# A mixture-of-experts dispatch on one NeuronCore: 128 blank rows behind each expert's last row instead of blank regions, and the early plan spread over the routing loop

## Chip and metric

The kernel runs on 1 NeuronCore of one Trainium2 chip. The metric is the device time of one execution in microseconds (us); the median of several runs is compared. Engines: TensorE (PE), VectorE (DVE), ScalarE (ACT), GpSimd (POOL); SyncE (SP) only issues transfers here.

## Reference

Two transformer layers on x of shape 16 x 256 x 128 (4096 tokens of 128 values). Only the last part bears on the change: a linear attention and then a layer of 16 experts, of which each token uses 2.

```python
# x = x + attention0(layernorm(x)); x = x + gated_recurrence0(layernorm(x))
# x = x + linear_attention1(layernorm(x)); x = x + moe1(layernorm(x))
logits = xt @ Wr + br                       # T = 4096 tokens, E = 16
w, idx = jax.lax.top_k(softmax(logits), 2)
w = w / jnp.clip(jnp.sum(w, axis=-1, keepdims=True), 1e-09)
comb = comb.at[jnp.arange(T)[:, None], idx].add(w)
h = gelu(jnp.einsum('td,edh->teh', xt, W1) + b1)   # hidden 256
o = jnp.einsum('teh,eho->teo', h, W2) + b2
y = xt + jnp.einsum('teo,te->to', o, comb)
```

## The kernel before

Every engine has its own program; semaphores order them. The trace has three stages: softmax attention and the recurrence (to about 303 us), linear attention with routing (to about 448 us), and the experts (from about 441 us to the end).

**Routing.** The loop of `linear_attention_and_routing` handles one block of 256 tokens per iteration n; the parts of an iteration belong to blocks n, n-2, n-3, n-5 and so on, so that 16 blocks take iterations 0 to 21 or 22. From n = 16 on, parts drop out (no more new blocks): this is the drain. DVE runs through a fixed order of small operations for each n; an iteration is counted below from its first operation in the steady state, `feat` (L1267). For each (token, choice) DVE computes a place in the DRAM tensor `disp`: expert e owns the region of 4224 rows from e*4224 on, and its rows are filled in order. POOL scatters the rows of a block there with 4 indirect transfers (L1209, tensor `pay`, a ring of `STORED` = 3; ACT may fill a slot of `pay` only when the scatter of three blocks ago has landed, L1420).

**Tiles.** The experts work on 80 tiles of 128 rows of `disp`, in 40 pairs. Which expert and which place a tile has stands in a table (`tablei`). Its first 16 tiles (pairs 0 to 7) are planned early, from the counts after block 9, and are full tiles only (`plan_early`, 19 dependent DVE steps in three lumps at the end of iterations 15, 16 and 17). The other 64 are planned when all blocks are counted (`plan_rest`, 18 dependent steps, line L1069 and on), from the counts rounded up: an expert's last tile reaches over its last row. The rows there must be blank (zero weight, and an index that is out of bounds, so that nothing is written back). Before the change SP fills all regions of `disp` with blank rows from the tile `fill` during routing: nine transfers (L1177), three in flight, and POOL waits for the one that covers a block before it scatters it.

**Experts.** For pair i SP loads a word of the table (L1705), takes two addresses from it and issues two transfers `rows<-disp` (L1718) into one of `R3` = 8 slots; slot i+8 also waits until pair i has been written back (`yout`). At i = 8 SP waits for the second part of the table, for all scatters and for the blank transfers. PE's step i is: turn the rows of pair i (L1828), the hidden layer of pair i-1 (L1832), the outputs of pair i-2 (L1839), in this order in one queue:

```python
        def step(i, k, r):
            if isinstance(i, int) and i == COPIED:
                before["rest_turned"](pe)
            turn(i, k, r)
            hidden(i, k, r)
            outputs(i, k, r)
```

DVE's step i copies the two experts' weights for pair i (`copy_own`, L1749) and multiplies the outputs of pair i-4 by their weights (L1767, called y below). POOL writes y back with one indirect transfer for each tile (L1688, 79 in all). When all are written back, SP reads them in order, DVE adds, and SP stores the result.

Of the kernel before, what the change touches and what calls it, by code (L numbers as in the profile page):

```python
# [13 lines left out]
P = 128  # L14
# [932 lines left out]
BLANK = 4  # L947
BLANKS = 3
N_BLANK = TOKENS // (BLANK * P) + 1
EARLY_STEPS = 19  # L950
R3 = 8
# [9 lines left out]
def linear_attention_and_routing(nc, ctx, t):  # L961
# [5 lines left out]
    with ExitStack() as scope:  # L967
# [69 lines left out]
        blank = [sig(f"blank{c}", 16) for c in range(BLANKS)]  # L1037
        t["blank"] = blank
# [27 lines left out]

        def count_tiles(then, dve, of, more, least):
# [12 lines left out]
        def place_tiles(then, dve, at):  # L1080

            then(dve.tensor_scalar(passed[:, 1:], tiles[0][:, lead:], w["iota_t"][:, 0:1], None, ALU.is_le))
            then(dve.tensor_reduce(at[:, 0:1], passed[:, 1:], AX.X, ALU.add))
            then(dve.tensor_tensor(which[:, :], passed[:, 0:E], passed[:, 1:], ALU.subtract))
            then(dve.tensor_tensor(which[:, :], which[:, :], offset[:, :], ALU.mult))
            then(dve.tensor_reduce(prevt[:, :], which[:, :], AX.X, ALU.add))
            then(dve.scalar_tensor_tensor(out=at[:, 1:2], in0=at[:, 0:1], scalar=float(STRIDE), in1=prevt[:, :], op0=ALU.mult, op1=ALU.add))
            then(dve.tensor_scalar(at[:, 1:2], at[:, 1:2], w["iota_t"][:, 0:1], float(E * STRIDE), ALU.add, ALU.min))
            then(dve.tensor_scalar(at[:, 0:1], at[:, 0:1], float(E - 1), None, ALU.min))
# [16 lines left out]
        def plan_early(dve, then, n):  # L1106

            if n == EARLY_OF + 5:
                dve.wait_ge(pos_s.sem, pos_s.at(EARLY_OF - 1, 1))
                dve.wait_ge(zeros_set.sem, zeros_set.at(0))  # L1110
                count_tiles(then, dve, place[(EARLY_OF - 1) % PAIR][:, TT, :], 0.0, 0.0)
            if n == EARLY_OF + 6:
                add_up(then, dve)
                then(dve.tensor_scalar(capped[:, :], tiles[0][:, lead - 1:], float(EARLY), None, ALU.min))
                then(dve.tensor_scalar(offset[:, :], tiles[0][:, lead - 1:lead - 1 + E], -1.0, None, ALU.mult))
            if n == EARLY_OF + 7:
                place_tiles(then, dve, here[0])
                then(dve.tensor_tensor(taken[:, :], capped[:, 1:], capped[:, 0:E], ALU.subtract))

        def plan_rest(dve):  # L1120

            then = stepper(dve, plan)
            dve.wait_ge(pos_s.sem, pos_s.at(B - 1))
            count_tiles(then, dve, counts, float(P - 1), float(P))
            then(dve.tensor_tensor(tiles[0][:, lead:], tiles[0][:, lead:], taken[:, :], ALU.subtract))
            add_up(then, dve)
            then(dve.tensor_tensor(offset[:, :], taken[:, :], tiles[0][:, lead - 1:lead - 1 + E], ALU.subtract))
            place_tiles(then, dve, here[1])
# [24 lines left out]
        def sums_free(dve):  # L1153
# [3 lines left out]
                       dict(pe=banks_free, dve=sums_free, rest=plan_rest, pack=pack_table, rest_turned=rest_turned))  # L1157
# [4 lines left out]
        def _(sp):  # L1162
# [20 lines left out]
        def _(pool):  # L1183
# [35 lines left out]
            def iteration(n, r):  # L1219
                o = 1 - r  # L1220
                root_power(n, r)
                if active(n, 5):
                    b = n - 5
                    if b * S % (BLANK * P) == 0:
                        c = b * S // (BLANK * P)
                        pool.wait_ge(blank[c % BLANKS].sem, blank[c % BLANKS].at(c // BLANKS))
                    pool.wait_ge(pos_s.sem, pos_s.at(b))
                    pool.wait_ge(ids_up.sem, ids_up.at(b))
                    for i in range(TT):
                        for k in range(TOP):  # L1230
                            scatter(b, i, k)
# [5 lines left out]
        def _(dve):  # L1237
# [11 lines left out]
            early_step = stepper(dve, early)  # L1249

            def iteration(n, r):
# [8 lines left out]
                if active(n, 3):  # L1260
# [4 lines left out]
                    if kv_p.due(b - PAIR):  # L1265
                        dve.wait_ge(kv_p.sem, kv_p.at(b - PAIR))
                    dve.scalar_tensor_tensor(out=feat[b % PAIR][:, :, :], in0=ex[:, :, :], scalar=1.0, in1=rl[:, :, :], op0=ALU.min, op1=ALU.add)\  # L1267
                        .then_inc(feat_s.sem, 1)
                if active(n, 6):
# [4 lines left out]
                if active(n, 2):  # L1274
                    b = n - 2
                    dve.wait_ge(qkv_p.sem, qkv_p.at(b))
                    if rot_s.due(b - 1):
# [5 lines left out]
                        .then_inc(t_s.sem, 1)  # L1283
                if active(n, 3):
# [18 lines left out]
                if active(n, 5):  # L1303
# [3 lines left out]
                                      wide(w["br"][:, :].rearrange("p (o e) -> p o e", o=1), [P, TT, E]), ALU.add).then_inc(lg_s.sem, 1)  # L1307
                if active(n, 3):
# [18 lines left out]
                if active(n, 5):  # L1327
                    b = n - 5
                    for i in range(TT):
                        dve.wait_ge(top_s.sem, top_s.at(b, 1 + i))  # L1330
                        dve.max_index(where[:, i, :], best[:, i, :], logits[:, i, :]).then_inc(top_s.sem, 1)
                if active(n, 2):
# [5 lines left out]
                if active(n, 5):  # L1338
# [4 lines left out]
                        .then_inc(hot_s.sem, 1)  # L1343
                if active(n, 5):
# [18 lines left out]
                if active(n, 5):  # L1363
                    b = n - 5
                    dve.wait_ge(pay_s.sem, pay_s.at(b, 1))
                    dve.reciprocal(z[:, :], z[:, :]).then_inc(pay_s.sem, 1)
                if active(n, 3):
# [16 lines left out]
                if active(n, 5):  # L1384
# [3 lines left out]
                    if b >= STORED:  # L1388
                        dve.wait_ge(sent[b % STORED].sem, sent[b % STORED].at(b // STORED - 1))
                    dve.tensor_tensor(pay[b % STORED][:, :, :, D], odds[:, :, :],  # L1390
                                      wide(z[:, :].rearrange("p (o i) -> p o i", o=1), [P, TOP, TT]), ALU.mult).then_inc(pos_s.sem, 1)
                if active(n, 3):
# [15 lines left out]
                plan_early(dve, early_step, n)  # L1408
# [204 lines left out]
def experts(nc, ctx, scope, t, banks, before):  # L1613
# [79 lines left out]
    def expert_sp(sp):  # L1693
# [3 lines left out]
        def step(i, k, r):  # L1697
# [191 lines left out]
def program(nc, x, Wqkv, bqk, bv, Wout, bout, gates_w, gates_u, gates_b, in_c, wo, uo, bo, Wqkv2, Wout2, Wr, br, W1, W2, b2, cosf, sinf, out):  # L1889
    with ExitStack() as ctx:  # L1890
# [21 lines left out]
        def neighbours(dst, src):  # L1912
# [10 lines left out]
                 fill=sb("fill", [P, BLANK, ROW]))  # L1923
# [48 lines left out]
```

## Time and profile before

| What | us |
|---|---|
| median of 3 runs | 579.33 (578.74 to 581.08) |
| the profiled execution | 580.04 |
| its span in the trace | 578.3 |
| DVE busy, 340 to 400 us | 57.26 of 60 |
| nine blank transfers, 4160 KB each but the last, issue to landing (median) | 38.4 |
| POOL's 79 write-backs | first at 450.79, last at 556.70 |

All times inside the kernel are us from the start of the span. The 1.74 us between the span and the profiled execution's own time lie around the span and are taken as constant. The share of busy time of an engine over the whole span says little here, since the three stages have different limits.

### The profile page before, as it was taken

Reading aid. Unit: us, or ns where it says so; the run is one execution under the profiler, and the core shown is the slowest. Engines: PE = TensorE matmul, PEld = TensorE weight load, DVE = VectorE, ACT = ScalarE, POOL = GpSimd, SP = SyncE. Lnnn points to the kernel's source line nnn. Section 1 sums busy time; section 2 is a strip of 40 time slices with the busy share of each in tenths; the row PEclk is TensorE's granted clock in tenths of the full one; section 3 lists DMA queues with packets and bytes.
Section 4 is the critical chain, followed back from the end, with each engine's and each line's share of the span. In section 5 each row is a group of like instructions: output and inputs, shape, how many; then the busy total and the mean of one; then the engine's idle time right before and its main releaser. Section 6 shows DMA issues by size and latency. Waiting matters only on the chain. (4 is left out here: it accounts for less than half of the span.)

```text
span 578.3 us, 13705 instructions
## 1 busy us (share of the span) xinstructions
PE 479.2 (83%) x4110; PEld 329.1 (57%) x4110; DVE 400.3 (69%) x957; ACT 345.1 (60%) x763; POOL 332.9 (58%) x484
## 2 busy tenths in 40 slices
PE   6667899999999999989886899998767988988700
PEld 5433455555555555544463666666456887887700
DVE  5776777877877777775144899999857885554306
ACT  2026777777777777767733678787535665555400
POOL 2544575565666666513214158888657677777740
PEclk8768999999999999999999999999956999999955
DMA  3575755343444433320009999999944233333229
GB/s 94 137 185 138 174 123 122 94 104 106 113 112 112 112 98 97 94 60 5 2 1 311 380 375 367 365 368 367 357 89 108 79 99 90 91 97 89 66 97 343
DMA packets 78749, 89.93 MB, mean 156 GB/s; under 512 B 8523, under 2 KB 56032, under 8 KB 78688
## 3 DMA queue, kind: packets, MB, share of 16 engines
q1 hardware_dynamic: 72424, 78.82, 46.5%
q0 software_dynamic: 4576, 8.47, 4.4%
q10 hardware_dynamic: 1688, 1.90, 1.4%
q8 instruction: 29, 0.48, 0.4%
q14 instruction: 32, 0.26, 0.2%
HBM read 30.40 MB, written 59.72 MB: 156 GB/s over the span
## 5 line engine op out<-in xcount | busy, mean ns | idle before, releaser
L576 ACT ACTIVATE probs<-p_exp 128x1024 f32<-128x1024 f32 x128 | 131.5, 1027 | 57.9 <-PE p_exp L680 57.3
L450 DVE TENSOR_REDUCE negmax<-p_max 128x4 f32<-128x1024 f32 x103 | 126.1, 1224 | 46.4 <-PE p_max L708 45.8
L1688 POOL DMA_INDIRECT back<-XN2T,rows x79 | 83.1, 1052 | 26.0 <-issue 21.0
L1209 POOL DMA_INDIRECT disp<-pay,pos x64 | 65.5, 1024 | 22.9 <-issue 21.8
L699 PE MATMUL p_out<-probs,V 128*32 128x256 f32 x1024 | 68.3, 385 | 0.0
L680 PE MATMUL p_exp<-QS,KS 64*128 64x256 bf16 x512 | 51.1, 278 | 8.5 <-ACT probs L576 5.3
L1811 ACT ACTIVATE hid<-p_qkv,own 128x128 f32<-128x128 f32 x158 | 45.3, 369 | 18.4 <-PE p_qkv L1832 17.4
L708 PE MATMUL p_max<-KS,QS 61*128 61x256 bf16 x412 | 41.4, 280 | 6.8 <-DMA QS<-scratch 3.8
L1749 DVE TENSOR_SCALAR own<-expert,every_bit 128x578 int32 x79 | 38.6, 531 | 9.9 <-issue 8.9
L680 PEld LDWEIGHTS p_exp<-QS,KS 64*128 64x128 bf16 x512 | 15.0, 94 | 52.6 <-ACT probs L576 30.8
L1832 PE MATMUL p_qkv<-XN2T,own 128*128 128x128 f32 x316 | 43.4, 281 | 0.1
L1217 POOL TENSOR_TENSOR roots<-roots,power 128x4 f32<-128x4 f32 x19 | 24.2, 1272 | 29.1 <-DVE roots L1407 28.5
L699 PEld LDWEIGHTS p_out<-probs,V 128*32 128x32 f32 x1024 | 26.8, 109 | 24.6 <-issue 13.5
L366 POOL CAST maxpart<-negmax 128x32 bf16<-128x32 f32 x16 | 3.4, 212 | 63.8 <-DVE negmax L450 63.8
L1832 PEld LDWEIGHTS p_qkv<-XN2T,own 128*128 128x128 f32 x316 | 39.5, 196 | 0.8 <-ACT XN2T L1801 0.5
L450 DVE TENSOR_REDUCE negmax<-p_small 128x4 f32<-128x1024 f32 x25 | 30.5, 1220 | 8.3 <-PE p_small L708 8.2
L708 PEld LDWEIGHTS p_max<-KS,QS 61*128 61x128 bf16 x412 | 16.6, 96 | 21.9 <-DVE negmax L450 15.0
L78 POOL TENSOR_TENSOR root<-root,power 128x2 f32<-128x2 f32 x32 | 22.5, 702 | 2.7
L385 POOL CAST part<-qk 128x512 bf16<-128x512 f32 x15 | 9.2, 611 | 21.3 <-ACT qk L587 21.3
L352 POOL TENSOR_TENSOR xn<-X,mv 128x256 f32<-128x256 f32 x30 | 18.5, 617 | 4.9 <-POOL root L78 2.0
L754 PE MATMUL p_misc<-xn1T,Wqk 128*128 128x256 f32 x64 | 19.7, 435 | 1.4 <-ACT V L616 0.9
L76 POOL TENSOR_SCALAR root<-mv 128x2 f32<-128x2 f32 x32 | 6.2, 193 | 24.7 <-DVE mv L442 24.6
(269 smaller groups left out, 1162.9 us busy)
## 6 DMA issues: line engine op xcount, KB each, us to landing
disp<-fill SPq DMA_DIRECT2D x8, 4160.0 KB, 38.4
scratch<-part SPq DMA_DIRECT2D x32, 192.0 KB, 2.1
KS<-scratch SPq DMA_DIRECT2D x32, 192.0 KB, 3.6
QS<-scratch SPq DMA_DIRECT2D x28, 192.0 KB, 4.5
rows<-disp SPq DMA_DIRECT2D x79, 65.0 KB, 1.8
scratch<-part SPq DMA_DIRECT2D x32, 128.0 KB, 1.9
own<-back SPq DMA_DIRECT2D x8, 512.0 KB, 8.2
expert<-in_W_dram SPq DMA_DIRECT2D x1, 2064.0 KB, 8.9
```

Of the source, the lines that this page charges most:

```text
L78: pool.tensor_tensor(y, v, t["power"][:, 0:TT], ALU.pow).then_inc(mark.sem, 1)
L450: dve.tensor_reduce(negmax[q][:, i, :, 2 * hp:2 * hp + 2], bank[:, :].rearrange("p (v w k) -> p v w k", v=HALF, k=S), AX.X, ALU.max, negat ...
L576: act.activation(probs[s % 4][:, :, :, :].rearrange("p v w q -> p (v w q)"), p_exp[:, :], ACT.Exp).then_inc(prob_s.sem, 1)
L680: mm = pe.matmul(p_exp[:, (2 * v + w) * S:(2 * v + w + 1) * S], KS[q][rows, h, kt * P:(kt + 1) * P], QS[q][rows, h, :], start=True, stop=True)
L699: mm = pe.matmul(p_out[32 * j:32 * j + 32, 0:S], values[:, first:first + 32], probs[s % 4][:, j % HALF, j // HALF, :], start=(s % 4 == 0), ...
L708: mm = pe.matmul(bank[:, (2 * v + w) * S:(2 * v + w + 1) * S], QS[q][rows, h, i * P:(i + 1) * P], KS[q][rows, h, :], start=True, stop=True)
L1209: pool.indirect_dma_start(out=disp, out_offset=bass.IndirectOffsetOnAxis(ap=pos[q][:, i, k:k + 1], axis=0), in_=pay[q][:, k, i, :], in_off ...
L1217: pool.tensor_tensor(root[m][:, 0, :], root[m][:, 2, :], t["power"][:, :], ALU.pow).then_inc(power_s.sem, 1)
L1688: pool.indirect_dma_start(out=back, out_offset=bass.IndirectOffsetOnAxis(ap=rows[r][:, h, D + 1:ROW].bitcast(U32), axis=0), in_=y[r][:, h, :],
L1749: done = dve.tensor_scalar(own[r][:, h, :].bitcast(I32), theirs, every_bit[:, 0:1], None, ALU.bitwise_and)
L1811: done = act.activation(hid[q][:, h, c, :], p_hid[q % 2][:, (2 * h + c) * P:(2 * h + c + 1) * P], ACT.Gelu, bias=own[q][:, h, HID + c:HID ...
L1832: return pe.matmul(dst, own[q][:, h, c * P:(c + 1) * P], xT[q][:, h * P:(h + 1) * P], start=True, stop=True)
```

## The change

1. The nine blank transfers during routing and POOL's waits for them are gone; `fill` holds one row per partition instead of four.
2. When all blocks are counted, DVE converts the 16 end positions to integers (`ends`). SP, after its transfers for pairs 0 to 7 and before that of pair 8, loads each end position into a register and writes 128 blank rows from there on: 16 loads and 16 transfers of 65 KB (`pads`). Pair 8 waits for all of them.
3. The 19 steps of the early plan are no longer in three lumps in which each step waits for the one before it; they stand one by one at 8 sites in iterations 15 to 17, and the wait for the step before stands at the next site.
4. The rest of the plan is cut in two: 9 steps before the expert loop of DVE, 9 in its step 4 behind y of pair 0, and `copy_own` of pair 4 behind them.

```diff
@@ SP, end of the set-up of the routing stage
-            blanks = disp[0:E * REGION, :].rearrange("(e r) d -> e r d", e=E)
-            for c in range(N_BLANK):
-                n = BLANK if c + 1 < N_BLANK else 1
-                if c >= BLANKS:
-                    sp.wait_ge(blank[c % BLANKS].sem, blank[c % BLANKS].at(c // BLANKS - 1))
-                sp.dma_start(blanks[:, c * BLANK * P:(c * BLANK + n) * P, :].rearrange("e (p n) d -> p e (n d)", n=n),
-                             w["fill"][:, 0:n, :].rearrange("p (o n) d -> p o (n d)", o=1).broadcast_to([P, E, n * ROW]))\
-                    .then_inc(blank[c % BLANKS].sem, 16)
@@ POOL, before the scatter of block b
-                    if b * S % (BLANK * P) == 0:
-                        c = b * S // (BLANK * P)
-                        pool.wait_ge(blank[c % BLANKS].sem, blank[c % BLANKS].at(c // BLANKS))
@@ SP, expert loop
             if isinstance(i, int) and i == R3:
+                sp.wait_ge(w["loaded3"].sem, w["loaded3"].at(0))
+                sp.wait_ge(t["ends_s"].sem, t["ends_s"].at(0))
+                for e in range(E):
+                    end = sp.value_load(t["ends"][0:1, e:e + 1], min_val=0, max_val=E * REGION - P)
+                    sp.dma_start(disp[bass.ds(end, P), :], w["fill"][:, 0, :]).then_inc(t["pads"].sem, 16)
                 sp.wait_ge(table.sem, 2)
...
             if isinstance(i, int) and i == R3:
-                sp.wait_ge(w["loaded3"].sem, w["loaded3"].at(0))
-                for c in range(N_BLANK - BLANKS, N_BLANK):
-                    sp.wait_ge(t["blank"][c % BLANKS].sem, t["blank"][c % BLANKS].at(c // BLANKS))
+                sp.wait_ge(t["pads"].sem, t["pads"].at(0))
@@ DVE, the rest of the plan
+        def plan_rest(dve, then, half):
+
+            if half == 0:
+                dve.wait_ge(pos_s.sem, pos_s.at(B - 1, 1))
+                dve.tensor_copy(ends[:, :], counts[0:1, :]).then_inc(ends_s.sem, 1)
+                count_tiles(then, dve, counts, float(P - 1), float(P))
+                then(dve.tensor_tensor(tiles[0][:, lead:], tiles[0][:, lead:], taken[:, :], ALU.subtract))
                 add_up(then, dve)
...
+            if half == 1:
+                then(dve.tensor_tensor(offset[:, :], taken[:, :], tiles[0][:, lead - 1:lead - 1 + E], ALU.subtract))
+                for step in range(8):
+                    place_tiles(then, dve, here[1], step)
@@ DVE, the sites of the early plan (eight calls of site(n, s) in an iteration)
+            def site(n, s):
+                if 0 <= (n - EARLY_OF - 5) * SITES + s < EARLY_STEPS:
+                    early_ready()
+                    plan_early(dve, early_step, n, s)
...
-                plan_early(dve, early_step, n)
+                site(n, 7)
@@ DVE, expert loop
-        before["rest"](dve)
+        rest = before["rest"](dve)
+        rest(0)
         before["dve"](dve)
 
         def step(i, k, r):
-            if i is not None and not (isinstance(i, int) and i < COPIED):
+            if i is not None and not (isinstance(i, int) and i <= COPIED):
                 copy_own(dve, i, k, r)
...
+            if isinstance(i, int) and i == COPIED:
+                rest(1)
+                copy_own(dve, i, k, r)
```

Instructions in order, SP before the change, from the second transfer of pair 7 to the first of pair 8 (`TENSOR_LOAD` loads a register from SBUF, `ISA` and `REGISTER_ALU` compute the address):

```order
L1718 DMA rows7<-disp 128x130
L1705 TENSOR_LOAD tablei [waits table]
L1705 ISA x2
L1718 REGISTER_ALU [waits sent1,sent0,sent2,blank2,yout0,blank1,loaded3,blank0]
L1718 ISA
L1718 DMA rows0<-disp 128x130
```

SP after the change, from the same place (line numbers are those of the changed kernel), the first two of the 16 blank transfers:

```order
L1757 DMA rows7<-disp 128x130
L1743 TENSOR_LOAD ends [waits ends_s,loaded3]
L1743 ISA x2
L1744 ISA
L1744 DMA disp<-fill 128x130
L1743 TENSOR_LOAD ends
L1743 ISA x2
L1744 ISA
L1744 DMA disp<-fill 128x130
```

and the last of them up to pair 8:

```order
L1743 TENSOR_LOAD ends
L1743 ISA x2
L1744 ISA
L1744 DMA disp<-fill 128x130
L1746 TENSOR_LOAD tablei [waits table]
L1746 ISA x2
L1757 REGISTER_ALU [waits sent2,yout0,sent1,pads,sent0]
L1757 ISA
L1757 DMA rows0<-disp 128x130
```

Sixteen loads with 16 transfers now stand between pairs 7 and 8.

DVE before the change, the end of iteration 17 and the `feat` that opens the next one:

```order
L1407 TENSOR_SCALAR roots<-mv 128x4 [waits st4]
L1082 TENSOR_SCALAR passed<-tiles,iota_t 128x16
L1083 TENSOR_REDUCE here<-passed 128x1 [waits early]
L1084 TENSOR_TENSOR which<-passed 128x16 [waits early]
L1085 TENSOR_TENSOR which<-which,offset 128x16 [waits early]
L1086 TENSOR_REDUCE prevt<-which 128x1 [waits early]
L1087 SCALAR_TENSOR_TENSOR here<-here,prevt 128x1 [waits early]
L1088 TENSOR_SCALAR here<-here,iota_t 128x1 [waits early]
L1089 TENSOR_SCALAR here<-here 128x1 [waits early]
L1118 TENSOR_TENSOR taken<-capped 128x16 [waits early]
L1267 SCALAR_TENSOR_TENSOR feat<-ex,rl 128x512 [waits qfT_p,kv_p,el_s,early]
```

DVE after the change, from the end of iteration 16 into iteration 17, where the last three steps of the early plan now stand:

```order
L1443 TENSOR_SCALAR roots<-mv 128x4 [waits st4]
L1101 SCALAR_TENSOR_TENSOR here<-here,prevt 128x1 [waits early]
L1296 SCALAR_TENSOR_TENSOR feat<-ex,rl 128x512 [waits kv_p,qfT_p,el_s]
L1103 TENSOR_SCALAR here<-here,iota_t 128x1 [waits early]
L1303 TENSOR_REDUCE pos<-mine 128x4 [waits pos_s]
L1311 TENSOR_TENSOR t<-p_qkv,cosf 128x512 [waits rot_s,qkv_p]
L1312 TENSOR_TENSOR t<-p_qkv,sinf 128x64x4
L1105 TENSOR_SCALAR here<-here 128x1 [waits early]
L1320 TENSOR_TENSOR KVm<-p_kvo,kv_mask 128x144 [waits o_p,kv_p]
```

The nine steps at the end of iteration 17 are gone from there; each of the moved ones has other work between it and the step on which it waits.

## Rows read from the trace of the kernel before

**Rows 1.** Windows: busy us of five engines, then TensorE clock, DMA share, GB/s
```profile
340.00:400.00 60.00, 55.53 (x323) 39.55 (x323) 57.26 (x256) 48.51 (x133) 49.48 (x46) 1.00 1.05 367
400.00:420.00 20.00, 14.60 (x85) 10.53 (x82) 17.06 (x83) 12.51 (x36) 13.77 (x14) 0.91 1.07 354
420.00:444.00 24.00, 16.27 (x74) 12.99 (x71) 15.87 (x86) 9.28 (x25) 14.75 (x16) 0.52 0.41 89
450.00:557.00 107.00, 86.28 (x732) 81.00 (x730) 57.42 (x147) 55.17 (x181) 82.43 (x79) 0.97 0.30 81
```

**Rows 2.** Timeline of VectorE: start us, us, engine, line, operation, out<-in
```profile
364.21 0.69 DVE L1267 SCALAR_TENSOR_TENSOR feat<-ex,rl 128x512 f32<-128x512 f32 x1
...
375.81 0.15 DVE L1350 TENSOR_TENSOR z<-odds 128x2 f32<-128x2 f32 x1
375.88 0.43 DVE L1356 BATCH_NORM_STATS2 mv<-X 128x6 f32<-128x256 f32 x1
...
398.12 0.69 DVE L1267 SCALAR_TENSOR_TENSOR feat<-ex,rl 128x512 f32<-128x512 f32 x1
...
405.69 0.17 DVE L1069 TENSOR_TENSOR full<-place,region 128x16 f32<-128x16 f32 x1
...
406.53 0.69 DVE L1267 SCALAR_TENSOR_TENSOR feat<-ex,rl 128x512 f32<-128x512 f32 x1
...
414.48 0.69 DVE L1267 SCALAR_TENSOR_TENSOR feat<-ex,rl 128x512 f32<-128x512 f32 x1
...
423.07 0.69 DVE L1267 SCALAR_TENSOR_TENSOR feat<-ex,rl 128x512 f32<-128x512 f32 x1
```

**Rows 3.** Waits, 340 to 400 us: us in total, times, longest
```profile
DVE den L1311 <- PE p_kvo L1578: 1.7, 9, 0.2
...
ACT pay L1421 <- DMA disp<-pay,pos: 0.5, 1, 0.5
```

**Rows 4.** Timeline of GpSimd at the end of dispatch and in the expert stage
```profile
447.64 0.96 POOL L1209 DMA_INDIRECT disp<-pay,pos  x1 [0.30 <-issue]
...
450.79 0.99 POOL L1688 DMA_INDIRECT back<-XN2T,rows  x1 [2.19 <-DVE XN2T L1767]
...
467.71 1.07 POOL L1688 DMA_INDIRECT back<-XN2T,rows  x1 [0.30 <-issue]
```

**Rows 5.** Timeline of VectorE: products y of pair 0 and of pair 6
```profile
449.51 0.42 DVE L1767 TENSOR_TENSOR XN2T<-p_kvo,rows 128x256 f32<-128x256 f32 x1
...
461.88 0.42 DVE L1767 TENSOR_TENSOR XN2T<-p_h,rows 128x256 f32<-128x256 f32 x1
```

**Rows 6.** Timeline of the SP queue, and line L1705 in 438 to 439
```profile
437.33 1.03 SPq L1718 DMA_DIRECT2D rows<-disp  x2
...
439.17 1.02 SPq L1718 DMA_DIRECT2D rows<-disp  x2
...
449.35 1.01 SPq L1718 DMA_DIRECT2D rows<-disp  x2
...
454.71 1.02 SPq L1718 DMA_DIRECT2D rows<-disp  x2
...
L1705 SPq TENSOR_LOAD <-tablei x1: 273/273/273, 438.4 to 438.4; - x1
```

**Rows 7.** Line L1718 (ns min/median/max), and the page's DMA issues
```profile
L1718 SPq DMA_DIRECT2D rows<-disp x79: 332/337/765, 435.4 to 540.0; - x79
...
rows<-disp SPq DMA_DIRECT2D x79, 65.0 KB, 1.8
```

**Rows 8.** Timeline of TensorE: turns of pairs 0 and 8, two hidden layers
```profile
440.81 0.66 PE L1828 MATMUL p_ta<-ident,rows 128*128 128x128 f32 x2 [0.71 <-DVE mine L1400]
...
442.00 2.07 PE L1832 MATMUL p_qkv<-XN2T,own 128*128 128x128 f32 x8
...
446.70 1.06 PE L1832 MATMUL p_qkv<-XN2T,own 128*128 128x128 f32 x8
...
459.17 0.38 PE L1828 MATMUL p_ta<-ident,rows 128*128 128x128 f32 x2
```

More of the change, by code:

```diff
@@ L946 @@
 PLACE_BITS = 10
[L947 to L949 removed]
 EARLY_STEPS = 19
+SITES = 8
 R3 = 8
@@ L1036, in linear_attention_and_routing @@
         table = t["table"]
-        blank = [sig(f"blank{c}", 16) for c in range(BLANKS)]
-        t["blank"] = blank
+        ends, ends_s, pads = tmp("ends", [1, E], I32), sig("ends_s"), sig("pads", 16 * E)
+        t["ends"], t["ends_s"], t["pads"] = ends, ends_s, pads
         fill_set, bsplit = sig("fill_set", 2), sig("bsplit", 6)
@@ L1065, in stepper, with spaced, then @@
             return then
+        def spaced(dve, mark):
+            n = [0]
+            def then(ins):
+                n[0] += 1
+                ins.then_inc(mark.sem, 1)
+            return then, lambda: n[0] and dve.wait_ge(mark.sem, n[0])
         def count_tiles(then, dve, of, more, least):
@@ L1078, in add_up, with place_tiles @@
                 then(dve.tensor_tensor(b[:, lead:], a[:, lead:], a[:, lead - s:lead - s + E], ALU.add))
[L1080 to L1089, printed above, removed]
+        def place_tiles(then, dve, at, step):
+            if step == 0:
+                then(dve.tensor_scalar(passed[:, 1:], tiles[0][:, lead:], w["iota_t"][:, 0:1], None, ALU.is_le))
+            if step == 1:
+                then(dve.tensor_reduce(at[:, 0:1], passed[:, 1:], AX.X, ALU.add))
+            if step == 2:
+                then(dve.tensor_tensor(which[:, :], passed[:, 0:E], passed[:, 1:], ALU.subtract))
+            if step == 3:
+                then(dve.tensor_tensor(which[:, :], which[:, :], offset[:, :], ALU.mult))
+            if step == 4:
+                then(dve.tensor_reduce(prevt[:, :], which[:, :], AX.X, ALU.add))
+            if step == 5:
+                then(dve.scalar_tensor_tensor(out=at[:, 1:2], in0=at[:, 0:1], scalar=float(STRIDE), in1=prevt[:, :], op0=ALU.mult, op1=ALU.add))
+            if step == 6:
+                then(dve.tensor_scalar(at[:, 1:2], at[:, 1:2], w["iota_t"][:, 0:1], float(E * STRIDE), ALU.add, ALU.min))
+            if step == 7:
+                then(dve.tensor_scalar(at[:, 0:1], at[:, 0:1], float(E - 1), None, ALU.min))
         def pack_table(dve, i, n):
@@ L1104, in pack_table, with plan_early @@
             dve.tensor_copy(tablei[:, :, i * EARLY:i * EARLY + n], tf[:, :, 0:n]).then_inc(table.sem, 1)
[L1106 to L1108 removed]
+        def plan_early(dve, then, n, site):
+            step = (n - EARLY_OF - 5) * SITES + site
+            if step == 0:
                 dve.wait_ge(pos_s.sem, pos_s.at(EARLY_OF - 1, 1))
                 dve.wait_ge(zeros_set.sem, zeros_set.at(0))
[L1111 to L1118 removed]
@@ L1120, in plan_rest @@
-        def plan_rest(dve):
-            then = stepper(dve, plan)
[L1123 to L1128, printed above, removed]
+                then(dve.tensor_tensor(full[:, :], place[(EARLY_OF - 1) % PAIR][:, TT, :], w["region"][:, :], ALU.subtract))
@@ new lines, in plan_early @@
+            if step == 1:
+                then(dve.tensor_scalar(counti[:, :], full[:, :], 0.0, 0.0, ALU.add, ALU.max))
+            if step == 2:
+                then(dve.tensor_scalar(counti[:, :], counti[:, :], 7, None, ALU.logical_shift_right))
+            if step == 3:
+                then(dve.tensor_copy(tiles[0][:, lead:], counti[:, :]))
+            if 4 <= step < 8:
+                a, b, s = tiles[step % 2], tiles[(step + 1) % 2], 1 << step - 4
+                then(dve.tensor_tensor(b[:, lead:], a[:, lead:], a[:, lead - s:lead - s + E], ALU.add))
@@ new lines, in plan_early @@
+            if step == 8:
+                then(dve.tensor_scalar(capped[:, :], tiles[0][:, lead - 1:], float(EARLY), None, ALU.min))
+            if step == 9:
+                then(dve.tensor_scalar(offset[:, :], tiles[0][:, lead - 1:lead - 1 + E], -1.0, None, ALU.mult))
+            if 10 <= step < 18:
+                place_tiles(then, dve, here[0], step - 10)
+            if step == 18:
+                then(dve.tensor_tensor(taken[:, :], capped[:, 1:], capped[:, 0:E], ALU.subtract))
+        def plan_rest(dve, then, half):
[4 more added lines that the diff above has]
+                then(dve.tensor_tensor(tiles[0][:, lead:], tiles[0][:, lead:], taken[:, :], ALU.subtract))
+                add_up(then, dve)
+            if half == 1:
+                then(dve.tensor_tensor(offset[:, :], taken[:, :], tiles[0][:, lead - 1:lead - 1 + E], ALU.subtract))
+                for step in range(8):
+                    place_tiles(then, dve, here[1], step)
@@ L1130, in rest_turned, with rest_planner @@
+        def rest_planner(dve):
+            then = stepper(dve, plan)
+            return lambda half: plan_rest(dve, then, half)
         def rest_turned(pe):
@@ L1922, in program @@
         w.update(expert=sb("expert", [P, E, EXPERT_ROW]), b_all=sb("b_all", [E, D]),
-                 fill=sb("fill", [P, BLANK, ROW]))
+                 fill=sb("fill", [P, 1, ROW]))
         w["bp"] = w["expert"][:, :, EXPERT:EXPERT_ROW]
```

11 lines of the change are left out of this document (9 added, 2 removed).

## Prediction

> **What bounds the kernel now.** I first read the windows, stage by stage. Between 340 and 400 us, the steady state of routing, DVE is busy for 57.26 of 60 us, and the DMA share is at its full value with 367 GB/s: the blank transfers fill the memory path, but DVE fills its own time too [rows 1]. So the second view is DVE's timeline. From the `feat` at 364.21 to that at 398.12 five iterations pass, (398.12 - 364.21)/5 = 6.78 us each [rows 2]. The third view is who waits for whom: in that stretch DVE waits 1.7 us in all, and for PE; the scatter's landing delays ACT once, by 0.5 us [rows 3]. Traffic is therefore nearly hidden in the steady state, and at most the 2.74 us that DVE is idle there could come back.
>
> Iterations 15 to 17 are longer: 398.12 to 406.53 (8.41 us), to 414.48 (7.95), to 423.07 (8.59) [rows 2]. They hold the lumps of 4, 6 and 9 plan steps. Between 420 and 444 us the granted clock is 0.52, the lower level (1.2 GHz) almost throughout, and PE is busy for only 16.27 of 24 us [rows 1]: a drain of dependent steps.
>
> In the expert stage POOL sets the pace. From 450 to 557 us it is busy for 82.43 us in 79 write-backs, 1.04 us each, with 0.3 us between two of them: 79 x 1.34 = 106 of 107 us [rows 1, 4]. PE is ahead of it: y of pair 6 ends at 461.88 + 0.42 = 462.30, and its first write-back starts at 467.71 [rows 4, 5]. What decides the end is thus when POOL starts, and whether it ever runs dry.
>
> **What the change gives back in routing.** A dependent plan step costs 0.21 us: four of them fill 405.69 to 406.53 [rows 2]. A small operation that waits for nothing moves the next one by 0.07 us (375.81 to 375.88) [rows 2]; I take 0.07 to 0.1 for a spread step, and nothing for the two sites in each iteration that stand ahead of a wait for PE.
> - Iteration 15: four steps (0.84) become eight spread ones, six of which count (0.6): 0.2 saved. Besides, 8.41 - 6.78 - 0.84 = 0.8 us are left, in which `pay` waits for its scatter and PE's work comes late; without the blank traffic I count that as saved.
> - Iteration 16: six steps (1.26) become eight (0.6): 0.7 saved.
> - Iteration 17: nine steps (1.9) become three (0.2): 1.7 less on DVE. PE and ACT have work of their own ahead of the next `feat`'s matmuls, so I take 1.5.
> - The drain: with shorter gaps PE may keep its high clock a little longer. The stretch of 24 us at the low clock [rows 1] is work of PE in about half of its chain; I estimate up to 2.5 us if the clock held, and take 0.6.
>
> Sum 0.8 + 0.2 + 0.7 + 1.5 + 0.6 = 3.8 us earlier at the end of routing. I call this X. Its bounds: 2.0 (late landing not cured, a spread step at nearly 0.2) and 5.8 (clock kept in the drain).
>
> The Trainium skill, "DMA: Bandwidth & Descriptors", section "Latency and other measured facts", puts the access latency of HBM far lower under light load than under heavy load. That speaks for the 0.8 us of iteration 15; the row itself shows only one wait of 0.5 us in 60 [rows 3], and by the row alone X would be 3.5.
>
> **The start of the write-backs.** The rest plan's cut lets y of pair 0 come before 9 of the steps and before the copy for pair 4. The last scatter ends at 447.64 + 0.96 = 448.60; the first write-back starts only at 450.79, behind y of pair 0, which ends at 449.51 + 0.42 = 449.93 [rows 4, 5]. It could start at about 448.9: 1.9 us more, if POOL then does not run dry.
>
> **What the change adds: 16 blank transfers in SP's queue.** All are issued by SP between pairs 7 and 8. SP takes 439.17 - 437.33 = 1.84 us for a pair with one table load and two transfers. The second transfer of a pair starts 1.02 - 0.34 = 0.68 us behind the first, so a load with its transfer takes 1.84 - 0.68 = 1.16 us; the load starts at 438.4 and its transfer at 439.17, 0.77 us later [rows 6, 7]. A blank transfer has one register operation less, about 0.04 us; on the other hand pairs 1 to 7 took (449.35 - 437.33)/6 = 2.0 us each instead of 1.84 [rows 6]. I take 1.12 us, within 1.02 (0.34 for the issue and 0.68 for the load) and 1.20. So 16 x 1.12 = 17.9 us.
>
> SP is done with pair 7 at 449.35 + 1.01 = 450.36 [rows 6]. Before, it then had a wait for the table and issued pair 8 at 454.71 [rows 6]. Now, in times of the old trace (X comes off at the end), the last blank transfer is issued at 450.4 + 17.9 - 0.4 = 467.9. A transfer of this size lands in 1.8 us [rows 7]; a write may take a little more. Landing 469.7, with 0.4 for address work pair 8 is issued at 470.1 and its rows are there at 471.9.
>
> The Trainium skill, on the same page and in the same section, gives a floor of about 0.6 us to a register load. With 0.34 us for the issue a blank transfer would be 0.94 us, the stop 2.9 us shorter, and the result some 582; the row's 0.77 us from load to transfer decides otherwise.
>
> **Who waits for pair 8.** PE's queue is in order: turn of 8, hidden of 7, outputs of 6. While PE waits for the rows of pair 8, y of pair 6 can't be made. Before, the turn of pair 8 started at 459.17 and y of pair 6 ended at 462.30, 3.13 us later [rows 5, 8]. Now 471.9 + 3.1 = 475.0. By then PE has been idle for some 15 us; after the poor stretch that ends at 440.81 the first hidden layer took 2.07 us at the low clock, later ones 1.06 [rows 8], so I add 1.5 us for the two passes: 476.5. POOL starts 450.79 - 449.93 = 0.86 us behind y [rows 4, 5]: write-back of pair 6 at 477.4 instead of 467.71. That is 9.7 us later. The remaining 67 write-backs follow without a gap as before, since PE and DVE are faster than POOL: by pair 6 they had gained 467.71 - 462.30 = 5.4 us on it [rows 4, 5]. The 1.9 us of the earlier first write-back are lost in the stall.
>
> **Sum.** 9.7 - 3.8 = +5.9 us. On the profiled execution's 580.04 that is 585.9; it lies 0.7 above the median, so the predicted median is 579.33 + 5.9 = 585.3 us, rounded up.
>
> **Rivals.**
> - *The blank transfers are cheap* and SP is through before POOL needs pair 6. Without a stall POOL wants pair 6 at 448.9 + (467.71 - 450.79) = 465.8; the gain is X + 1.9 = 5.7: 573.6 us, faster. It needs 465.8 instead of 477.4, thus 11.6/16 less for each transfer: 0.40 us. The sign turns at 1.12 - 5.9/16 = 0.75 us. For it: the issue alone is 0.34 us. Against it: every transfer has its own load in front, and those took 0.77 us. Chance 0.08.
> - *The blank traffic held routing back more than the waits show.* DVE could win at most its idle time, 2.74 us in 60, some 3 over the loaded stretch: 582.3 us, at the edge of what can be told. Against it: DVE is full. Chance 0.12.
> - *The blank transfers are dearer*: writes of 128 short rows that come every 1.1 us back up, or the cold PE falls behind POOL for several pairs. At 1.4 us each, +4.5: 590 us. Chance 0.10.
> - *My forecast*, a stall at pair 8 less X: 0.70.
>
> **Numbers.** A measurement of this kernel tells about 0.5%, 2.9 us, from no change. The forecast's own range is from +1.5 (X 5.8, 1.05 us each, PE not cold) to +9.5 (X 2.0, 1.2 us each): 581 to 589. That also takes in the second rival; outside are the first, the third and some 0.02 of the others, so this is the range. Faster by over 0.5%: 0.08 and a little of the second rival's tail, 0.09. Within: half of the second rival and 0.11 of the forecast, 0.17. Slower: 0.74.
>
> **What the changed kernel's profile would show.** SP: 16 pairs of load and transfer, about 1.1 us apart, for some 18 us, and pair 8 issued around 466. POOL: write-backs of pairs 0 to 5 without a gap from about 445 on, then idle for some 10 us ahead of pair 6. PE: idle for about 15 us, then hidden layers of 2 us at clock 0.5. DVE: iterations 16 and 17 near 7.2 and 6.9 us, plan steps not back to back. DMA from 320 to 420 us nearly empty, and iterations of still 6.8 us there. The prediction is wrong if SP takes well under 0.75 us for a blank transfer, or if iterations before 14 get shorter.

## The result and the profile after

| What | us |
|---|---|
| kernel before, median of 7 runs | 579.56 (578.74 to 584.32) |
| changed kernel, median of 7 runs | 586.28 (583.54 to 587.52) |
| ratio, 95% interval | 1.0095 (1.0066 to 1.0124) |
| profiled execution of the changed kernel, its span | 583.54, 581.6 |

By the ratio the change made the kernel slower by 5.5 us (0.0095 x 579.56), between 3.8 and 7.2; the two medians stand 6.7 us apart. The profiled execution of the changed kernel is the fastest of its seven. Everything ahead of routing is unchanged code and ended 2.7 us earlier in this trace than in that of before (DVE's first instruction of the stage at 300.41 and 303.06), so I count from the first `feat` of each trace: 316.62 before, 313.94 after.

Windows of the changed kernel, the same four stretches and columns as [rows 1]:

```profile
340.00:400.00 60.00, 55.48 (x325) 39.80 (x323) 57.53 (x260) 48.20 (x133) 49.07 (x45) 1.00 0.12 39
400.00:420.00 20.00, 14.87 (x84) 11.31 (x83) 16.33 (x86) 12.71 (x34) 16.82 (x15) 0.87 0.13 41
420.00:444.00 24.00, 19.04 (x107) 15.85 (x106) 16.00 (x86) 11.45 (x34) 16.91 (x18) 0.61 0.33 87
450.00:557.00 107.00, 84.34 (x706) 80.86 (x704) 54.20 (x133) 53.27 (x176) 74.87 (x72) 0.93 0.31 84
```

In the first one the memory path is nearly empty now (39 GB/s instead of 367), and DVE is as busy as before. In the last one POOL is busy for 7.6 us less: it stood still. The stretches lie at fixed times, and the changed kernel reaches the end of routing some 7 us earlier in its trace, so the third one holds more of its expert stage and can't be compared column by column.

VectorE's timeline, the last four `feat` (L1296), answers to [rows 2]:

```profile
395.44 0.69 DVE L1296 SCALAR_TENSOR_TENSOR feat<-ex,rl 128x512 f32<-128x512 f32 x1
402.46 0.69 DVE L1296 SCALAR_TENSOR_TENSOR feat<-ex,rl 128x512 f32<-128x512 f32 x1
409.30 0.68 DVE L1296 SCALAR_TENSOR_TENSOR feat<-ex,rl 128x512 f32<-128x512 f32 x1
416.06 0.69 DVE L1296 SCALAR_TENSOR_TENSOR feat<-ex,rl 128x512 f32<-128x512 f32 x1
```

Iterations 15 to 17 take 7.02, 6.84 and 6.76 us instead of 8.41, 7.95 and 8.59: 4.33 us less. Up to 395.44 all iterations have kept their length (81.50 us from the first `feat` in both traces).

The SP queue (SPq: transfers that SP issues; ACTq below: those of ScalarE), timeline, and the loads of the end positions (ns min/median/max), answer to [rows 6]:

```profile
428.37 15.16 SPq L1757 DMA_DIRECT2D rows<-disp  x16
444.36 16.85 SPq L1744 DMA_DIRECT2D disp<-fill  x16
463.14 7.12 SPq L1757 DMA_DIRECT2D rows<-disp  x8
...
L1743 SPq TENSOR_LOAD <-ends x16: 262/271/356, 443.6 to 460.2; - x16
```

The 16 blank transfers follow the pairs 0 to 7 at once, (16.85 - 0.33)/15 = 1.10 us apart. Pair 8 is issued 19.6 us behind the end of pair 7.

TensorE at the outputs of pair 2 and at the end of the stall, VectorE's y of pair 6, timelines, answer to [rows 5, 8]:

```profile
445.90 0.29 PE L1879 MATMUL p_h<-own,ones 128*128 128x128 bf16 x1 [1.76 <-DVE tablef L1112]
...
465.92 0.69 PE L1871 MATMUL p_ta<-ident,rows 128*128 128x128 f32 x2 [10.64 <-DMA rows<-disp]
466.40 1.91 PE L1875 MATMUL p_qkv<-XN2T,own 128*128 128x128 f32 x8
...
470.10 0.42 DVE L1807 TENSOR_TENSOR XN2T<-p_h,rows 128x256 f32<-128x256 f32 x1 [12.20 <-PE p_h L1882]
```

GpSimd, timeline, answers to [rows 4]: the last scatter, the first write-backs of pairs 0, 1 and 2, and those of pair 6.

```profile
440.61 0.96 POOL L1236 DMA_INDIRECT disp<-pay,pos  x1 [0.30 <-issue]
441.88 1.00 POOL L1724 DMA_INDIRECT back<-XN2T,rows  x1 [0.30 <-issue]
...
446.46 0.98 POOL L1724 DMA_INDIRECT back<-XN2T,rows  x1 [2.29 <-DVE XN2T L1807]
...
449.56 0.98 POOL L1724 DMA_INDIRECT back<-XN2T,rows  x1 [0.84 <-DVE XN2T L1807]
...
471.34 1.19 POOL L1724 DMA_INDIRECT back<-XN2T,rows  x1 [10.75 <-DVE XN2T L1807]
...
474.16 0.98 POOL L1724 DMA_INDIRECT back<-XN2T,rows  x1 [0.30 <-issue]
```

The chain of the stall is to be read in these three views: SP issues pair 8 at 463.14, TensorE has waited 10.64 us for its rows, behind that turn in TensorE's queue stands what y of pair 6 needs (DVE waits 12.20), and POOL waits 10.75. Counted from the first `feat`:

| From the first `feat`, us | before | after | difference |
|---|---|---|---|
| last scatter starts | 131.02 | 126.67 | -4.35 |
| first write-back | 134.17 | 127.94 | -6.23 |
| write-back of pair 6 | 151.09 | 157.40 | +6.31 |
| last write-back (559.96 after) | 240.08 | 246.02 | +5.94 |

### The profile page after: what moved, and what is told of

Its sections match the earlier page's. It is cut to its first block and busy times, and to the rows that moved or that the text cites. A ratio compares the mean times of both kernels' runs of the same rounds, so it can differ in the third digit from the quotient of the medians.

```text
span 581.6 us, 13792 instructions
## 1 busy us (share of the span) xinstructions
PE 480.5 (83%) x4110; PEld 332.7 (57%) x4110; DVE 399.6 (69%) x958; ACT 344.3 (59%) x763; POOL 333.5 (57%) x484
## 5 line engine op out<-in xcount | busy, mean ns | idle before, releaser
L1788 DVE TENSOR_SCALAR own<-expert,every_bit 128x578 int32 x79 | 39.8, 546 | 9.6 <-issue 8.5
L1875 PE MATMUL p_qkv<-XN2T,own 128*128 128x128 f32 x316 | 45.1, 289 | 0.1
L1875 PEld LDWEIGHTS p_qkv<-XN2T,own 128*128 128x128 f32 x316 | 41.6, 205 | 0.5 <-ACT XN2T L1844 0.5
L385 POOL CAST part<-qk 128x512 bf16<-128x512 f32 x15 | 9.1, 609 | 19.6 <-ACT qk L587 19.6
L1844 ACT ACTIVATE XN2T<-p_ta 128x256 f32<-128x256 f32 x20 | 7.7, 384 | 21.2 <-issue 15.3
```

Of the source, the lines that this page charges most:

```text
L1788: done = dve.tensor_scalar(own[r][:, h, :].bitcast(I32), theirs, every_bit[:, 0:1], None, ALU.bitwise_and)
L1875: return pe.matmul(dst, own[q][:, h, c * P:(c + 1) * P], xT[q][:, h * P:(h + 1) * P], start=True, stop=True)
```

## Experiments

All are compared with the kernel before, run on the same chip in turn with them. Times "from the first `feat`" are from the one profiled execution.

**The plan alone** (e1_plan_only): the changed kernel, with the nine blank transfers and POOL's waits as before and no `pads`.

```diff
-                for e in range(E):
-                    end = sp.value_load(t["ends"][0:1, e:e + 1], ...)
-                    sp.dma_start(disp[bass.ds(end, P), :], w["fill"][:, 0, :]).then_inc(t["pads"].sem, 16)
+            # the nine transfers of the kernel before, ahead of the expert loop
```

> The blank transfers of before are kept; only the plan is spread and cut. If the loss of the change lies in SP's 16 transfers and its gain in the plan's steps, this has the gain alone: the changed kernel's routing ended 4.3 us earlier counted from the start of its stage, of which 3.5 are the plan's, and the write-backs follow POOL, so about 576 us against 579.6 (ratio 0.993). If instead the removed blank traffic brought the gain, this stays at 579.6. If the cut of the rest plan is what delays the experts, this is slower than before.

Measured 576.88 us against 579.28, ratio 0.9959 (0.9929 to 0.9989): the plan is the part that gains. Its last three iterations, and one wait of ScalarE (timelines):

```profile
398.25 0.69 DVE L1309 SCALAR_TENSOR_TENSOR feat<-ex,rl 128x512 f32<-128x512 f32 x1
405.27 0.69 DVE L1309 SCALAR_TENSOR_TENSOR feat<-ex,rl 128x512 f32<-128x512 f32 x1
412.11 0.68 DVE L1309 SCALAR_TENSOR_TENSOR feat<-ex,rl 128x512 f32<-128x512 f32 x1
418.85 0.69 DVE L1309 SCALAR_TENSOR_TENSOR feat<-ex,rl 128x512 f32<-128x512 f32 x1
...
419.91 0.21 ACT L1470 ACTIVATE pay<-ids 128x4 int32<-128x4 int32 x1 [1.79 <-DMA disp<-pay,pos]
```

The iterations are those of the changed kernel (7.02, 6.84, 6.74), with full blank traffic beside them. But one iteration later `pay` waits 1.79 us for a scatter that lands late, and from there on the trace is 1.9 us behind the changed kernel: the last scatter starts 128.54 us from the first `feat` (126.67 there). So of X = 4.35 us the spread plan gives 2.5 with the blank traffic beside it, and taking the traffic away then gives 1.9 more. Its last write-back starts 236.24 us from the first `feat`, 3.8 less than before. A difference of 2 us between two single traces is not safe by itself: the changed kernel, e5_half_on_act, e10_interleaved_again and e11_bare_again have the last scatter at 126.60 to 126.69, but e3_twice, with the same routing code, at 128.79. What carries the 1.9 us here is the wait of 1.79 us in the trace.

**The blank rows alone** (e2_lumps): the changed kernel with the early plan in its three lumps.

```diff
-                if 0 <= (n - EARLY_OF - 5) * SITES + s < EARLY_STEPS:
-                    early_ready()
-                    plan_early(dve, early_step, n, s)
+                if s == SITES - 1 and n in LUMPS:          # {15: (0, 4), 16: (4, 10), 17: (10, 19)}
+                    for step in range(*LUMPS[n]):
+                        plan_early(dve, early_step, EARLY_OF + 5, step)
```

> The changed kernel with the early plan back in three lumps of dependent steps at the ends of iterations 15, 16 and 17. By my theory the plan's spread gives 3.5 us and the stall at pair 8 moves with the end of routing: 586.3 + 3.5 = 589.8 us (ratio to before 1.017). If the blank traffic's end brought the gain, 586.

Measured 592.0 us, ratio 1.0205 (1.0165 to 1.0245). Iterations 15 to 17 took 7.59, 7.94 and 9.06 us, the last scatter started 130.61 us from the first `feat`, and the last write-back 249.79: 3.8 us behind the changed kernel, as expected. In this order the split of X is another one: without the plan's spread the empty memory path gives 0.4 us (131.02 to 130.61), since iteration 15 is 0.82 us shorter than before but iteration 17 is 0.47 us longer, and the spread then gives 3.9. What is shown is that the spread is the larger part, 2.5 to 3.9 us of 4.35, and that the two parts do not add up one by one. The medians stand 6 us apart; the rest of it lies ahead of the first `feat` in the trace (below) and isn't explained for the medians.

**Twice as many** (e3_twice): 16 more loads with transfers, to the 128 rows behind the blank ones.

```diff
+                for e in range(E):
+                    end = sp.value_load(t["ends"][0:1, e:e + 1], ...)
+                    sp.dma_start(disp[P:, :][bass.ds(end, P), :], w["fill"][:, 0, :]).then_inc(t["pads"].sem, 16)
```

> The changed kernel with every load and blank transfer issued twice, the second 128 rows further on, 32 in all. If SP's issue time is fully on the path, each costs the 1.10 us that stands between two of them in the trace: 16 x 1.1 = 17.6 us more, 604 us (ratio 1.042). If the delay at pair 8 had another cause (the landing of the last, the table), little is added: 586 to 588.

Measured 605.12 us, ratio 1.0442 (1.0394 to 1.0491), 18.8 above the changed kernel's median, 1.18 for each. SP's and POOL's timelines:

```profile
447.05 16.80 SPq L1744 DMA_DIRECT2D disp<-fill  x16
464.63 17.17 SPq L1747 DMA_DIRECT2D disp<-fill  x16
483.36 16.36 SPq L1760 DMA_DIRECT2D rows<-disp  x15
...
491.91 1.19 POOL L1724 DMA_INDIRECT back<-XN2T,rows  x1 [30.34 <-DVE XN2T L1810]
```

POOL's stall is 19.6 us longer: 30.34 instead of 10.75 us. In the queue itself each of the 16 more costs 1.10 us again: from the first blank transfer to pair 8 it is 36.31 us (447.05 to 483.36) instead of 18.78, 17.5 us more. From the first `feat` to the last write-back the trace is 19.7 us longer; 2.1 us of that lie ahead of the last scatter, in code that did not change, and why is open.

**Transfers without a load** (e9_bare, e11_bare_again): 16 more behind the 16, to fixed rows of a tensor of their own.

```diff
+                for e in range(E):
+                    sp.dma_start(t["spare"][e * P:(e + 1) * P, :], w["fill"][:, 0, :]).then_inc(t["pads"].sem, 16)
```

> The changed kernel with 16 more transfers of 128 rows in SP's queue behind the 16 blank ones, without a register load, to fixed rows of a tensor of their own. With load and register address 16 more cost 18.8 us, 1.18 each. Theory: the load (0.77 us from load to transfer) is the larger part, and a bare transfer costs the issue alone, 0.34 us: +5.4 us over the changed kernel, 591.7. Rival: the transfers themselves back up, because a write of 128 rows takes about 1.1 us of the queue: +18, 604.

> The kernel of e9_bare once more, for the same reason. Theory: 16 bare transfers cost 0.34 us each, +5.4 over the changed kernel, 591.7. Rival: they cost about 1.1 us each as the ones with a load do, +18, 604.

In the first comparison the kernel before itself took 627.33 us, and this one 642.63: ratio 1.023 (1.0178 to 1.0281). In the second they took 581.13 and 594.83, ratio 1.0236 (1.0196 to 1.0277), 8.2 us above the changed kernel's 1.0095. SP's and POOL's timelines of the second, and the row of line L1746:

```profile
445.76 16.82 SPq L1744 DMA_DIRECT2D disp<-fill  x16
462.62 8.29 SPq L1746 DMA_DIRECT2D spare<-fill  x16
473.65 26.14 SPq L1759 DMA_DIRECT2D rows<-disp  x22
...
482.12 1.19 POOL L1724 DMA_INDIRECT back<-XN2T,rows  x1 [19.99 <-DVE XN2T L1809]
...
L1746 SPq DMA_DIRECT2D spare<-fill x16: 320/432/936, 462.6 to 470.5; - x16
```

A bare transfer costs (8.29 - 0.4)/15 = 0.53 us in the queue, more than the 0.34 of a single issue (the longest was 0.94), and half of the 1.10 with a load. Neither expectation was met exactly; the load with its address work is about half of the price, not two thirds. (The bare ones also go to another tensor; whether that matters was not tested.)

**Eight of them on ScalarE** (e5_half_on_act).

```diff
-                for e in range(E):
+                for e in range(0, E, 2):
@@ ScalarE, at the end of its step i
+            if isinstance(i, int) and i < E // 2:
+                if i == 0:
+                    act.wait_ge(t["ends_s"].sem, t["ends_s"].at(0))
+                end = act.value_load(t["ends"][0:1, 2 * i + 1:2 * i + 2], ...)
+                act.dma_start(disp[bass.ds(end, P), :], w["fill"][:, 0, :]).then_inc(t["pads"].sem, 16)
```

> Half of the loads and blank transfers are issued by ScalarE, one in each of its steps 0 to 7; SP issues the other eight. By my theory SP reaches pair 8 8.8 us earlier, and POOL's idle time ahead of pair 6 falls from 10.8 us to 2 or less: 577.5 us (ratio 0.996). If the landing or PE's low clock holds pair 6 back, or ScalarE's steps become the limit (1.1 us more in each), 582 to 586.

Measured 584.49 us, ratio 1.0066 (1.004 to 1.0092): my expectation of a gain fell, and the time lies where its rivals had put it (582 to 586). SP's, ScalarE's and POOL's timelines:

```profile
449.26 8.36 SPq L1744 DMA_DIRECT2D disp<-fill  x8
465.02 34.84 SPq L1757 DMA_DIRECT2D rows<-disp  x29
...
462.90 0.34 ACTq L1865 DMA_DIRECT2D disp<-fill  x1
...
473.08 1.19 POOL L1724 DMA_INDIRECT back<-XN2T,rows  x1 [5.34 <-DVE XN2T L1807]
```

SP was through at 457.6, but ScalarE's steps are paced by TensorE and its last transfer came at 462.90; pair 8 waited for that one. The stall is halved, and the wait for the counts in ScalarE's step 0 took part of it back in front of pair 0 (POOL idle 2.54 us there, 0.30 in the changed kernel).

**The same 16, only those that are needed ahead of pair 8** (e8_interleaved, e10_interleaved_again). Pair 8 needs the blank rows of the first experts alone.

```diff
@@ SP, at pair 8
-                for e in range(E): (load and transfer)
+                for e in range(4): (load and transfer)
@@ SP, behind the transfers of pairs 8 to 14
+            if isinstance(i, int) and R3 <= i < R3 + 7:
+                pad(sp, 4 + i - R3, t["more"][(i - R3) % 2])
@@ ScalarE, at the end of steps 4 to 8
+                pad(act, 11 + i - 4, t["by_act"])
```

> The changed kernel with the same 16 blank transfers placed otherwise: SP issues 4 before pair 8 and one behind each of pairs 8 to 14, ScalarE issues 5 in its steps 4 to 8; pair 8 waits only for the first 4, each later pair for those of two pairs before. (The order holds for the counts of these inputs; for all inputs it would need a guard.) Theory: what costs is that 16 transfers stand in one queue ahead of pair 8, 12 of them without need; pair 8 is then issued some 12 us earlier than in the changed kernel, POOL's idle time before pair 6 falls from 10.75 us to under 1, and the routing gain is left: 586.3 - 10 = 576, up to 578 if SP, at 2.9 us for each of pairs 8 to 14 against POOL's 2.68, falls behind. Rival: the blank transfers cost where the write meets the scatters and reads in the DMA queues, wherever they are issued; then the time stays over 582.

> The kernel of e8_interleaved once more, because in that comparison the kernel before itself took 627 us instead of 579 and POOL was no longer what sets the pace of the expert stage. Where the kernel before takes about 579: theory, POOL's idle time before pair 6 under 2 us instead of 10.75 and 576 to 578 us. Rival: the blank transfers still hold up something else that shares their queues, and the time stays over 582.

The first comparison is the one with 627.33 us for the kernel before: this one took 627.64, ratio 0.9995 (0.9956 to 1.0033). POOL did not set the pace there, but against the changed kernel with its rest plan uncut, run beside it (e7_rest_uncut, 637.44), it is 9.8 us faster. In the second: 577.55 us against 581.13, ratio 0.9937 (0.991 to 0.9964), 9 us below the changed kernel's ratio. SP's and POOL's timelines:

```profile
449.62 3.80 SPq L1733 DMA_DIRECT2D disp<-fill  x4
455.46 1.07 SPq L1766 DMA_DIRECT2D rows<-disp  x2
457.31 0.35 SPq L1733 DMA_DIRECT2D disp<-fill  x1
458.55 1.02 SPq L1766 DMA_DIRECT2D rows<-disp  x2
...
452.38 0.98 POOL L1726 DMA_INDIRECT back<-XN2T,rows  x1 [2.72 <-DVE XN2T L1821]
455.46 0.98 POOL L1726 DMA_INDIRECT back<-XN2T,rows  x1 [0.80 <-DVE XN2T L1821]
458.32 0.99 POOL L1726 DMA_INDIRECT back<-XN2T,rows  x1 [0.59 <-issue]
```

Behind pair 3 POOL has no idle time over 0.45 us left, and the last write-back (554.72) starts 235.49 us from the first `feat`: 4.6 less than before, 10.5 less than in the changed kernel. The same work in other places of the queues turns a loss into a gain, for these inputs: with other counts a later pair could read its rows before they are blank, and a guard against that was not built. Its lead over the plan alone (0.9959) lies within the intervals.

**The cut of the rest plan** (e6_spread_only and e12_spread_only_again: the kernel before with the early plan spread, nothing else; e7_rest_uncut: the changed kernel with the rest plan in one piece; e13_interleaved_uncut: the interleaved kernel likewise).

```diff
-        rest(0)
+        rest(0)
+        rest(1)
@@ step
-            if isinstance(i, int) and i == COPIED:
-                rest(1)
-                copy_own(dve, i, k, r)
```

> The kernel before with the early plan spread and nothing else: blank transfers during routing kept, the rest plan in one piece. Theory: the spread alone saves 2.5 us of routing (1.4 in iteration 15, 1.1 in 16, 1.8 in 17, and 1.8 given back where a late scatter holds the pay of a later block, as the trace of the kernel with plan alone shows); the cut of the rest plan only brought the first write-back 1.9 us forward. So the last scatter starts 128.5 us after the first feat (before: 131.0), the first write-back 131.7 after it (before: 134.2), and the time is 2.5 us under the kernel before: 577. Rival: the cut of the rest plan is what gave the gain at the end; then the time is within 1 us of before, 579.

> The changed kernel with the rest plan in one piece again. Theory: the end is set by pair 8, whose rows wait for the 16 blank transfers, and these wait only for the counts (ends), which come before the rest plan; so the first write-back is 1.9 us later, the stall before pair 6 1.9 us shorter, and the time is the changed kernel's, 586, within 1 us. Rival: the cut itself costs time (TensorE's table matmul and the wait for tablef stand in the middle of the first pairs); then the time falls by 1 to 3 us, to 583 to 585.

> The kernel of e6_spread_only once more, where the kernel before takes about 579: the early plan spread, blank transfers during routing and the rest plan as before. Theory: 2.5 us of routing are saved (last scatter 128.5 us after the first feat instead of 131.0) and the cut of the rest plan is worth little, since POOL waits 2.3 us before pair 1 with it: 577, as with the plan alone (576.9 against 579.3, ratio 0.996). Rival: the cut carried the gain; then within 1 us of the kernel before.

> The kernel of e8_interleaved with the rest plan in one piece. Theory: the cut only moves POOL's wait from ahead of pair 0 to ahead of pair 1, so the time stays within 1.5 us of the interleaved kernel's ratio 0.994 to before, and POOL's idle time before pairs 0, 1 and 2 together is 2 to 4 us as it is there. Rival: the first write-back 1.9 us later is passed on to the end; then 1.9 us slower, ratio 0.997.

All four ran where the kernel before takes 627 us, so the times expected don't apply, only the ratios. Spread alone: 0.995 (0.9915 to 0.9984) and 0.9924 (0.9892 to 0.9955), no worse than with the cut (0.9959). Interleaved and uncut: 0.9981 (0.9948 to 1.0015), beside 0.9995 with the cut in such a comparison. Changed kernel uncut: 637.44 us, 1.0172 (1.0127 to 1.0216), with POOL idle for 14.43 us ahead of pair 6; the changed kernel was not run there, so this says nothing of the cut. In the traces of the interleaved kernel there, POOL waits 4.18 us ahead of pair 0 without the cut (2 to 4 expected) and 2.29, 2.72 and 0.84 us ahead of pairs 0, 1 and 2 with it; from the last scatter to the last write-back it is 140.94 and 140.41 us. In none of these is a gain of the cut to be seen; a value under 2 us stays open.

## Why the prediction was right, and where its terms were off

- **Sum**: +5.9 predicted, +5.94 from the first `feat` to the last write-back, +5.5 (3.8 to 7.2) by the ratio, +6.7 between the medians. Predicted 585.3 us, measured 586.28. The mechanism was right; that the trace agrees to 0.04 us is luck, since three errors cancel: the stall is 1.0 us longer than predicted, X is 0.55 larger, and from the write-back of pair 6 to the last one it is 88.62 us instead of 88.99.
- **The range**: by its own terms its ends are 9.7 - 1.1 - 1.5 - 5.8 = +1.3 and 9.7 + 1.3 - 2.0 = +9.0, not +1.5 and +9.5. The result lies inside either.
- **X**, 3.8 predicted, 4.35 measured. Iteration 15 gave 1.39 (1.0 predicted), 16 gave 1.11 (0.7), 17 gave 1.83 (1.5): a spread step is nearly free (iterations 15 and 16 with eight each are 0.24 and 0.06 us over 6.78) where I had charged 0.07 to 0.1. The term for the drain was wrong: 0.6 predicted, and last iterations and drain took the same time in both (4.35 of the gain against 4.33 from the three iterations; 24.57 and 24.55 us from the last `feat` to the last scatter). The hope was that TensorE keeps its high clock longer, and it did not: over just this stretch the granted clock is 0.56 before (423.07 to 447.64) and 0.54 after (416.06 to 440.61).
- **The 0.8 us of the late landing** was put down to blank traffic. e2_lumps shows it: 7.59 instead of 8.41 us without the traffic. e1_plan_only shows that the spread plan alone also reaches 7.02, but then the wait comes up later, with 1.79 us. The two parts of the change are not additive in that term. A scatter lands 6.4 us after its issue in the kernel before, 6.5 in e1_plan_only and 2.4 in the changed kernel (medians). The Trainium skill, "DMA: Bandwidth & Descriptors", section "Latency and other measured facts", has HBM access latency grow with load; these rows agree in direction.
- **The blank transfers**, 1.12 us each predicted, 1.10 measured; pair 8 19.7 us behind the end of pair 7 predicted, 19.6 measured. The Trainium skill, "DMA: Bandwidth & Descriptors", section "Latency and other measured facts", has a floor of about 0.6 us for a register load, and the estimate from it, 0.94, would have been too low; the queue's row decided rightly. Its two halves were misjudged (0.77 for the load; e11_bare_again leaves 0.57), with no effect on the sum.
- **From pair 8 to POOL**, 7.3 us predicted (470.1 to 477.4), 8.2 measured (463.14 to 471.34): the hidden layer at the low clock (granted 0.50 from 466 to 468 us) took 1.91 us, and turn and y together 1.5 us more than before, as expected, but the turn started 2.8 us behind the issue of pair 8 and not 1.8: it waits for both transfers of the pair, and the second starts 0.68 us behind the first, which I had left out. TensorE was idle for 10.64 us and not for some 15, with no effect on the sum. The stall against the kernel before is thus 10.7 us and not 9.7, and that more than cancels the larger X.
- **The first write-back** came 1.88 us closer behind the last scatter (1.9 predicted), but write-backs without a gap up to pair 5 was wrong: TensorE waits 1.76 us for `tablef`, and POOL stands for 2.29 and 0.84 us ahead of pairs 1 and 2. I had not followed the table's own small steps into TensorE's queue. The stall hides this in the changed kernel.
- **Rivals.** Cheap transfers: fell by 1.10 us against the turning point at 0.75; a bare one at 0.53 would have been under it. Routing held back by traffic: fell for the steady state (6.78 us with 39 GB/s too); at its end it cost 0.4 us beside the lumps and 1.9 beside the spread plan. Dearer transfers: 1.10 us apart at 32 of them too, so no.

## What to carry to other kernels

Here the blank writes cost 0.4 to 1.9 us while they had SP's queue to themselves, and their whole length where they stood in order ahead of the one transfer on which the next stage hangs. So count loads and transfers of that queue up to there, and issue only as many as the next reader needs. A short transfer whose address is loaded from SBUF takes 1.1 us of its queue here, 16 of them 17 us. Taking a load off the memory path (367 to 39 GB/s) gave back only what some engine really waited for.

## What was not expected of the hardware

**The start of routing has two lengths.** From the stage's first DVE instruction to the first `feat` it is 13.5 us in 8 of the 14 traces (before 303.06 to 316.62, after, e3_twice and others) and 16.0 to 17.1 in 6 (e1_plan_only, e2_lumps and e5_half_on_act among them), with the same code. Windows of two us, e1_plan_only first:

```profile
306.00:308.00 2.00, 1.82 (x4) 1.40 (x5) 0.73 (x3) 0.70 (x2) 1.01 (x1) 0.55 1.09 357
308.00:310.00 2.00, 1.53 (x5) 0.78 (x4) 0.00 (x0) 0.75 (x2) 0.00 (x0) 0.50 1.10 354
310.00:312.00 2.00, 2.00 (x5) 0.97 (x4) 0.00 (x0) 0.00 (x0) 0.00 (x0) 0.50 1.09 352
```

and the changed kernel:

```profile
306.00:308.00 2.00, 1.53 (x7) 1.13 (x8) 0.46 (x2) 0.84 (x3) 1.01 (x1) 1.00 1.09 357
308.00:310.00 2.00, 1.47 (x6) 0.66 (x4) 0.71 (x2) 0.01 (x1) 0.00 (x0) 1.00 1.10 352
```

TensorE's granted clock fell to 0.50 there in the one and stayed at 1.00 in the other, and the start is 2.4 to 3.6 us longer with it; which of the two causes the other was not tested. In all 6 long ones it was below 0.7 between 308 and 310 us, in all 8 short ones 1.00. Part of the spread of the medians may come from it; one profile of each kernel can't tell how often.

**The same kernel at 627 us.** In two comparisons the kernel before took 627 us instead of 579. Routing began at 301 us as elsewhere (e6_spread_only), but its iterations from 342 us on took 8.5 us instead of 6.78 (`feat` at 342.02, 350.55, 359.04), with DVE waiting 1.3 to 1.4 us for TensorE in each of the two. Without blank traffic they are as long (e8_interleaved, 8.45 to 8.55 us), and the granted clock from 342 to 384 us is 1.00 in e12_spread_only_again, 0.96 in e6_spread_only and 0.92 in e8_interleaved, so neither the traffic nor the clock explains them. The cause is open.
